# Three fp16 products of a value block: three matmuls of 128 columns into one PSUM region, in place of one of 256 and one of 128

## The chip, the cores and the metric

The kernel runs on one core of a Trainium2 chip. The metric is the device time of one execution in microseconds (us), from the first to the last instruction of that core and what the runtime puts around it; less is better. TensorE is PE in the profile (PEld is its weight loads), VectorE is DVE, ScalarE is ACT, GpSimd is POOL, and SP issues the transfers.

## The reference

Two layers of graph attention on 3125 nodes with 128 features, 103125 edges, then a residual and a layer norm. Of one layer (4 heads in the first, 2 in the second, 128 features per head):

```python
q = (x @ Wq + bq).reshape(n, H, C)
k = (x @ Wk + bk).reshape(n, H, C)
v = (x @ Wv + bv).reshape(n, H, C)
alpha = jnp.einsum('ehc,ehc->eh', q[dst], k[src]) / jnp.sqrt(jnp.float32(C))
amax = jax.ops.segment_max(alpha, dst, num_segments=n)
p = jnp.exp(alpha - amax[dst])
denom = jax.ops.segment_sum(p, dst, num_segments=n) + 1e-16
out = jax.ops.segment_sum(p[:, :, None] * v[src], dst, num_segments=n)
out = out / denom[:, :, None]
return out.reshape(n, H * C) + x @ Ws + bs      # second layer: the mean over heads
```

The last step is `_layernorm(x + layer2(relu(layer1(x))))`.

## The kernel before

**Stages.** The kernel turns the edge list into a dense additive mask of 3125 x 3125 (the logarithm of the edge count), stored in DRAM (`mask_and_projections`, to 612 us of the span). `attention` then runs for layer 1 (612 to 1800 us), `projections2` between (1800 to 1925), `attention` for layer 2 (1925 to 2558), and `layer_norm` last.

**Attention.** Nodes are cut into NT = 25 tiles of TP = 125. For a tile of targets t and a head h, called head step s = t * H + h (100 of them in layer 1, 50 in layer 2), the 3125 sources are cut into NP = 7 pieces: six of 500 (four tiles) and one of 125 (one tile). For each piece PE makes the scores (three fp16 products of high and low parts, L1239), DVE adds the mask and takes the maximum (L1133), ACT takes the exponential (L1077), PE transposes the probabilities tile by tile (L1264, fp32), ACT writes their high fp16 part (L1084), DVE their low part (L1145), and PE sums the values (`values`, L1268 to L1279). So there are 25 value tiles in a head step, 3750 in all, in 1050 blocks of four tiles or of one.

**Precision.** K, V, the queries and the probabilities are held as a high and a low fp16 part. Of a product of two such pairs three terms are kept: high x high, high x low, low x high. In `values` the first matmul has the high probabilities as its weights and the high and low V side by side as 256 moving columns (L1275), so that high x high goes to columns 0 to 127 of the PSUM bank `O` and high x low to columns 128 to 255. The second has the low probabilities as weights and the high V as 128 moving columns (L1277), into columns 0 to 127. Each `pe.matmul` is a weight load of 125 columns and a matmul. There is one bank `O`: the first value block of a head step waits for `s_sum` of the step before (L1271).

**After the seven pieces** DVE runs `value_sum` (L1166): it waits for the last value matmul, copies the low half of `O` to `summed` (L1170, semaphore `s_low`) and adds the high half (L1172, `s_sum`). POOL multiplies by `v_back`, the powers of two that undo the scaling of V (L1038, `s_back`), then by the softmax weight (L1041), and adds the skip rows (L1047, or L1050 and L1053 in layer 2).

**What sets the order.** Each engine's order is written out by hand in its `tile` function, one step k = 0..6 per piece. PE issues in a step: the scores of the piece k + 5, the transposes of the piece k + 2 (both ahead, into the next head steps), then the values of piece k. DVE issues: mask and maximum of the piece k + 5, at k = 6 `value_sum`, then the low part of the piece k + 2, then small softmax operations. `over_tiles` (L958) runs the first tile, then a hardware loop of 11 passes with two tiles in each (L961), then the last two tiles. The waits are semaphores; none of the other ones is touched.

Of the kernel before, what the change touches and what calls it, by code (L numbers as in the profile page):

```python
# [22 lines left out]
ALU = mybir.AluOpType  # L23
# [5 lines left out]
TP = 125  # L29
NT = N // TP  # L30
C = 128
# [50 lines left out]
def wait(eng, sem, value):  # L82

    if not (isinstance(value, int) and value <= 0):
        eng.wait_ge(sem, value)


def tiles_of(p):

    return range(PIECES[p][0] // TP, PIECES[p][1] // TP)  # L90


def build(nc, x, src, dst, Wq1, bq1, Wk1, bk1, Wv1, bv1, Ws1, bs1,
# [4 lines left out]
    with ExitStack() as ctx:  # L98
# [6 lines left out]
        with ExitStack() as lay:  # L105
            def sb1(name, shape, dt=F32):
                return lay.enter_context(nc.sbuf_tensor(name, shape, dt))

            layer1 = {
                "featT": sb1("xT", [C, NT, 1, TP]),  # L110
                "KT": sb1("KT1", [C, H1, 2, N], F16),
                "V": sb1("V1", [TP, NT, H1, 2, C], F16),
                "v_back": sb1("v_back1", [C, H1 * C]),
                "Wq": sb1("Wq1_sb", [C, 1, H1 * C]),
                "Ws": sb1("Ws1_sb", [C, 1, H1 * C]),
                "bq": sb1("bq1_sb", [C, H1]),
                "bs": sb1("bs1_sb", [TP, H1 * C]),
            }
            mask_and_projections(nc, x, src, dst, Wk1, bk1, Wv1, bv1, Wq1, bq1, Ws1, bs1, bs2,
                                 ident, xres, layer1, mask_dram)  # L120
            attention(nc, 1, H1, 1, layer1, mask_dram, ident, hT_dram=hT_dram, h_max=h_max)
# [783 lines left out]
def attention(nc, layer, H, KC, L, mask_dram, ident, hT_dram=None, h_max=None, xres=None, y=None, stats=None):  # L905
# [3 lines left out]
    featT, KT, V, v_back, Wq, Ws, bq = (L[n] for n in ("featT", "KT", "V", "v_back", "Wq", "Ws", "bq"))  # L909
    W = H * C if layer == 1 else C  # L910
    with ExitStack() as ctx:
        def sb(name, shape, dt=F32):
            return ctx.enter_context(nc.sbuf_tensor(f"{name}_l{layer}", shape, dt))

        def bank(name):
            return ctx.enter_context(nc.psum_tensor(f"{name}_l{layer}", [C, 512], F32))

        def sem(name):
            return ctx.enter_context(nc.semaphore(f"{name}_l{layer}"))
# [16 lines left out]
        summed = sb("summed", [TP, 2, C])  # L936
# [3 lines left out]
        O, B_q, B_skip = bank("output"), bank("query"), bank("skip_rows")  # L940
# [6 lines left out]
        s_max, s_exp = sem("max_ready"), sem("exp_ready")  # L947
        s_tp, s_hi, s_t = sem("transposed_in_psum"), sem("probT_hi_ready"), sem("probT_ready")
        s_pv = sem("values_summed")
        s_sum, s_back, s_wtd, s_out = (sem(n) for n in ("sum_ready", "sum_scaled_back", "sum_weighted", "rows_ready"))  # L950
        s_low, s_pool_seen, s_top = sem("sum_low_ready"), sem("pool_seen"), sem("largest_taken")
        s_sp, s_skip = sem("skip_in_psum"), sem("skip_ready")
        s_rp, s_r, s_stored = sem("rowsT_in_psum"), sem("rowsT_ready"), sem("rowsT_stored")
        s_tot, s_w0, s_w1, s_w2 = (sem(n) for n in ("total_ready", "denom_ready", "inverse_ready", "weight_ready"))
# [3 lines left out]
        def over_tiles(eng, body):  # L958

            body(0, 0, 0)  # L960
            with eng.Fori(0, (NT - 3) // 2) as i:  # L961
                body(2 * i + 1, i, 1)
                body(2 * i + 2, i + 1, 0)
            body(NT - 2, (NT - 2) // 2, 1)
            body(NT - 1, (NT - 1) // 2, 0)
# [4 lines left out]
        def exists(t):  # L970
            return not isinstance(t, int) or t < NT

        def ahead(t, h, n):

            return t + (h + n) // H, (h + n) % H
# [13 lines left out]
        with nc.Block() as block:  # L989
            @block.sync  # L990
            def _(sp):
                def load_mask(t, parity):
                    for r0, r1 in ROW_SPLIT:
                        sp.dma_start(mask[r0:r1, parity, :], mask_dram[bass.ds(t * TP + r0, r1 - r0), :]
                                     ).then_inc(s_mask[parity], 16)

                def store_rowsT(t):
                    sp.wait_ge(s_r, t + 1)
                    sp.dma_start(hT_dram[bass.ds(t, 1)].rearrange("a p n -> (a p) n"), rowsT[:, :]).then_inc(s_stored, 16)

                def tile(t, i, parity):
                    if exists(t + 2):
                        sp.wait_ge(s_masked, NP * H * (t + 1))
                        load_mask(t + 2, parity)
                    if layer == 1:
                        store_rowsT(t)

                for n, (a, b) in enumerate(FIRST):
                    for r0, r1 in ROW_SPLIT:
                        sp.dma_start(mask[r0:r1, 0, a:b], mask_dram[r0:r1, a:b]).then_inc(s_first[n], 16)  # L1010
                load_mask(1, 1)
                over_tiles(sp, tile)
                if layer == 1:
                    sp.wait_ge(s_stored, 16 * NT)

            @block.gpsimd
            def _(pool):
                def query_parts(n, u):

                    pool.wait_ge(s_qs, n + 1).then_inc(s_pool_seen, 1)
                    pool.tensor_copy(QT[:, u, 0, :], q_now[:, u, :]).then_inc(s_qh, 1)  # L1023
                    pool.wait_ge(s_qh, n + 1)
                    pool.tensor_tensor(QT[:, u, 1, :], q_now[:, u, :], QT[:, u, 0, :], ALU.subtract).then_inc(s_q, 1)

                def tile(t, i, parity):
                    wait(pool, s_sp, t)
                    pool.tensor_copy(feat_now[:, :, :].rearrange("c k n -> c (k n)"),
                                     featT[:, bass.ds(t, 1), :, :].rearrange("c a k n -> c (a k n)")).then_inc(s_feat, 1)  # L1030
                    for h in range(H):
                        s = t * H + h
                        if exists(ahead(t, h, 3)[0]):
                            query_parts(s + 3, (h + 3) % 2)

                        o = summed[:, h % 2, :]
                        pool.wait_ge(s_sum, s + 1)
                        pool.tensor_tensor(o, o, v_back[0:TP, h * C:(h + 1) * C], ALU.mult).then_inc(s_back, 1)  # L1038
                        pool.wait_ge(s_w2, s + 1)
                        pool.wait_ge(s_back, s + 1).then_inc(s_pool_seen, 1)  # L1040
                        pool.tensor_scalar(o, o, weight[:, h % 2:h % 2 + 1], None, ALU.mult).then_inc(s_wtd, 1)  # L1041
                        pool.wait_ge(s_skip, t + 1)
                        pool.wait_ge(s_wtd, s + 1)
                        if layer == 1:
                            if h == 0:
                                wait(pool, s_rp, t)
                            pool.tensor_tensor(rows[:, h * C:(h + 1) * C], o, skip[:, h * C:(h + 1) * C],  # L1047
                                               ALU.add).then_inc(s_out, 1)
                        elif h == 0:
                            pool.tensor_tensor(rows[:, :], o, skip[:, :], ALU.add).then_inc(s_out, 1)  # L1050
                        else:
                            pool.wait_ge(s_out, s)
                            pool.tensor_tensor(y[:, bass.ds(t, 1), :].rearrange("p a c -> p (a c)"), o, rows[:, :],  # L1053
                                               ALU.add).then_inc(s_out, 1)

                for n in range(3):
                    query_parts(n, n % 2)
                over_tiles(pool, tile)

            @block.scalar  # L1060
# [56 lines left out]
            def _(dve):  # L1117
# [48 lines left out]
                def value_sum(s, h):  # L1166

                    dve.wait_ge(s_pv, NP * (s + 1))
                    wait(dve, s_out, s - 1)
                    dve.tensor_copy(summed[:, h % 2, :], O[0:TP, C:2 * C]).then_inc(s_low, 1)  # L1170
                    dve.wait_ge(s_low, s + 1)
                    dve.tensor_tensor(summed[:, h % 2, :], O[0:TP, 0:C], summed[:, h % 2, :], ALU.add).then_inc(s_sum, 1)  # L1172

                def largest_features(t):
                    dve.wait_ge(s_r, t + 1)
# [45 lines left out]
            def _(pe):  # L1221
# [46 lines left out]
                def values(s, p, h):  # L1268
                    pe.wait_ge(s_t, NP * s + p + 1)
                    if p == 0:  # L1270
                        wait(pe, s_sum, s)  # L1271
                    for i, t in enumerate(tiles_of(p)):
                        hi, lo = (probT[:, p, n, i * TP:(i + 1) * TP] for n in range(2))

                        pe.matmul(O[0:TP, 0:2 * C], hi, V[:, t, h, :, :].rearrange("p a c -> p (a c)"),  # L1275
                                  start=t == 0, stop=False, skip_group_check=True)
                        last = pe.matmul(O[0:TP, 0:C], lo, V[:, t, h, 0, :], start=False, stop=t == NT - 1,  # L1277
                                         skip_group_check=True)
                    last.then_inc(s_pv, 1)  # L1279
# [93 lines left out]
```

## Time and profile before

| | |
|---|---|
| time, median of 3 runs | 2584.7 us (2581.99 to 2587.41) |
| span of the profiled execution | 2580.9 us |
| mean granted PE clock | 0.978 |
| PE, PEld busy | 2360.8, 2004.2 us |
| DVE, ACT, POOL busy | 2026.2, 1651.1, 433.0 us |
| attention, layer 1 and layer 2 | 612 to 1800 us and 1925 to 2558 us |
| `values`: matmuls of 256 and of 128 columns | 3750 and 3750 |
| value matmuls' busy time | 739.8 and 680.9 us |

The page gives no time of its own for the profiled execution beside the span; the median of the runs is 3.8 us above the span. PE's busy time counts pipelined matmuls that overlap, so the cost of a matmul is read from the distance between two starts, not from its duration.

### The profile page before, as it was taken

Reading aid. Unit: us, or ns where it says so; the run is one execution under the profiler, and the core shown is the slowest. Engines: PE = TensorE matmul, PEld = TensorE weight load, DVE = VectorE, ACT = ScalarE, POOL = GpSimd, SP = SyncE. Lnnn points to the kernel's source line nnn. Section 1 sums busy time; section 2 is a strip of 40 time slices with the busy share of each in tenths; the row PEclk is TensorE's granted clock in tenths of the full one; section 3 lists DMA queues with packets and bytes.
Section 4 is the critical chain, followed back from the end, with each engine's and each line's share of the span. In section 5 each row is a group of like instructions: output and inputs, shape, how many; then the busy total and the mean of one; then the engine's idle time right before and its main releaser. Section 6 shows DMA issues by size and latency. Waiting matters only on the chain. (4 is left out here: it accounts for less than half of the span.)

```text
span 2580.9 us, 64168 instructions
## 1 busy us (share of the span) xinstructions
PE 2360.8 (91%) x18557; PEld 2004.2 (78%) x18558; DVE 2026.2 (79%) x6021; ACT 1651.1 (64%) x3383; POOL 433.0 (17%) x876
## 2 busy tenths in 40 slices
PE   2778888887999999999999999998789999999995
PEld 1356666666888888888888888888468999999995
DVE  5699999997888878888878878887237777777775
ACT  1689999995666666666666666665116665566653
POOL 4410000000211111121212111121011121211211
PEclk8889999999999999999999999999899999999998
DMA  2012222223211211112112112110312221222210
GB/s 71 1 59 87 87 86 86 86 86 93 54 31 33 55 34 36 48 34 54 30 34 54 30 34 54 33 31 9 134 42 68 63 73 48 73 60 61 73 48 26
DMA packets 46697, 141.98 MB, mean 55 GB/s; under 512 B 7621, under 2 KB 22828, under 8 KB 40249
## 3 DMA queue, kind: packets, MB, share of 16 engines
q1 hardware_dynamic: 43103, 136.94, 19.1%
q10 hardware_dynamic: 3396, 2.42, 0.4%
q8 instruction: 121, 1.98, 0.3%
q14 instruction: 77, 0.63, 0.1%
HBM read 91.34 MB, written 48.00 MB: 54 GB/s over the span
## 5 line engine op out<-in xcount | busy, mean ns | idle before, releaser
L1084 ACT ACTIVATE probT_l<-transposed_l 125x500 f16<-125x500 f32 (+1 forms) x1050 | 569.7, 543 | 669.5 <-PE transposed_l L1264 655.2
L1133 DVE CUSTOM_DVE_ANT_0 prob_l<-score_l,mask_l 125x500 f32<-125x500 f32 (+1 forms) x1050 | 649.8, 620 | 256.1 <-PE score_l L1239 210.6
L1239 PE MATMUL score_l<-KT,QT_l 128*125 128x500 f16 (+1 forms) x3150 | 771.1, 354 | 24.1 <-issue 17.6
L1145 DVE SCALAR_TENSOR_TENSOR probT_l<-transposed_l,probT_l 125x500 f16<-125x500 f32 (+1 forms) x1050 | 651.0, 620 | 125.4 <-ACT probT_l L1084 119.3
L1275 PE MATMUL output_l<-V,probT_l 125*125 125x256 f16 x3750 | 739.8, 275 | 0.0
L1277 PE MATMUL output_l<-V,probT_l 125*125 125x128 f16 x3750 | 680.9, 219 | 0.0
L1264 PEld LDWEIGHTS transposed_l<-ident,prob_l 125*125 125x125 f32 x3750 | 549.5, 188 | 91.8 <-DVE probT_l L1145 6.7
L1264 PE MATMUL transposed_l<-ident,prob_l 125*125 125x125 f32 x3750 | 589.5, 275 | 5.0 <-DVE probT_l L1145 5.0
L1077 ACT ACTIVATE prob_l<-prob_l,neg_max_l 125x1000 f32<-125x1000 f32 (+1 forms) x450 | 521.5, 1159 | 0.0
L1275 PEld LDWEIGHTS output_l<-V,probT_l 125*125 125x125 f16 x3750 | 512.3, 137 | 9.7 <-issue 0.2
L1277 PEld LDWEIGHTS output_l<-V,probT_l 125*125 125x125 f16 x3750 | 516.9, 138 | 0.0
L739 PE MATMUL mask_banks<-hot,work 125*125 125x313 bf16 x2432 | 388.4, 307 | 66.6 <-DVE hot L646 66.2
L1239 PEld LDWEIGHTS score_l<-KT,QT_l 128*125 128x125 f16 x3150 | 347.9, 138 | 113.6 <-issue 36.0
L739 PEld LDWEIGHTS mask_banks<-hot,work 125*125 125x125 bf16 x2432 | 278.8, 136 | 158.7 <-DVE hot L646 67.1
L646 DVE TENSOR_SCALAR hot<-cols,col_of 125x626 bf16<-125x626 f16 x960 | 316.3, 371 | 1.4 <-PE mask_banks L739 1.4
L1023 POOL CAST QT_l<-q_now_l 128x125 f16<-128x125 f32 x150 | 43.8, 292 | 1276.0 <-ACT q_now_l L1064 1276.0
L416 ACT ACTIVATE row_diff<-rows,minus_rel 125x125 bf16<-125x125 f16 x640 | 211.0, 389 | 8.9 <-DVE minus_rel L633 6.8
L1038 POOL TENSOR_TENSOR summed_l<-summed_l,v_back 125x128 f32<-125x128 f32 x150 | 68.2, 455 | 595.6 <-DVE summed_l L1172 595.6
L426 ACT ACTIVATE work<-row_diff,one 125x250 bf16<-125x250 bf16 x320 | 151.5, 494 | 0.0
L644 DVE TENSOR_SCALAR work<-rows,row_of,base 125x250 bf16<-125x250 f16 (+1 forms) x320 | 105.2, 329 | 0.9 <-PE mask_banks L739 0.9
L624 DVE SCALAR_TENSOR_TENSOR work<-mask_banks,work 125x626 f32<-125x626 f32 x128 | 101.6, 794 | 1.8 <-ACT work L400 1.8
L400 ACT ACTIVATE work<-mask_banks,tiny 125x626 f32<-125x626 f32 x128 | 98.6, 770 | 4.0 <-PE mask_banks L748 3.5
(176 smaller groups left out, 1723.2 us busy)
## 6 DMA issues: line engine op xcount, KB each, us to landing
mask_l<-mask_scratch SPq DMA_DIRECT2D x48, 1367.2 KB
mask_scratch<-work SPq DMA_DIRECT2D x128, 273.4 KB
mask_l<-mask_scratch SPq DMA_DIRECT2D x48, 158.7 KB
hT_scratch<-rowsT_l SPq DMA_DIRECT2D x25, 250.0 KB, 2.2
hT<-hT_scratch SPq DMA_DIRECT2D x6, 1000.0 KB, 13.5
mask_scratch<-work SPq DMA_DIRECT2D x128, 31.7 KB
mask_l<-mask_scratch SPq DMA_DIRECT2D x2, 929.7 KB
xres<-in_x SPq DMA_DIRECT2D x1, 1562.5 KB
```

The costliest lines, as they stand in the source:

```text
L416: last = act.activation(row_diff[:, n % 3, start:end], rows[:, cut], ACT.Square, bias=minus_rel[:, u, k:k + 1])
L426: act.activation(row_buffer[:, start:start + width(n)], row_diff[:, n % 3, 0:width(n)], ACT.Relu, bias=one[:, 0:1], scale=-1.0).then_inc(s ...
L646: dve.tensor_scalar(col_hot[:, k % RING, :], cols[:, :], col_w[:, k:k + 1], BIG, ALU.is_equal, ALU.mult).then_inc(s_hot, 1)
L739: ins = pe.matmul(counts(u, v)[:, a, :], one_hot, col_hot[:, hot, a * HB:(a + 1) * HB], start=k == (0, KF1)[v], stop=False, skip_group_che ...
L1077: act.activation(e, e, ACT.Exp, bias=neg_max[:, h % 2:h % 2 + 1], accum_out=total[:, h % 2, c:c + 1]).then_inc(s_exp, 1)
L1084: act.activation(probT[:, p, 0, 0:b - a], flip_bank(h, p)[0:TP, 0:b - a], ACT.Copy, scale=P_UP).then_inc(s_hi, 1)
L1133: dve.tensor_tensor_reduce(out=prob[:, h % 2, a:b], in0=score_bank(h, p)[0:TP, 0:b - a], in1=mask[:, parity, a:b], scale=1.0, scalar=-3.0e ...
L1145: dve.scalar_tensor_tensor(probT[:, p, 1, 0:b - a], flip_bank(h, p)[0:TP, 0:b - a], P_UP, probT[:, p, 0, 0:b - a], ALU.mult, ALU.subtract) ...
L1239: last = pe.matmul(score_bank(h, p)[0:TP, 0:b - a], QT[:, h % 2, i, :], KT[:, h, j, a:b], start=n == 0, stop=n == len(parts) - 1)
L1264: last = pe.transpose(flip_bank(h, p)[0:TP, i * TP:(i + 1) * TP], prob[:, h % 2, t * TP:(t + 1) * TP], ident[0:TP, 0:TP])
L1275: pe.matmul(O[0:TP, 0:2 * C], hi, V[:, t, h, :, :].rearrange("p a c -> p (a c)"), start=t == 0, stop=False, skip_group_check=True)
L1277: last = pe.matmul(O[0:TP, 0:C], lo, V[:, t, h, 0, :], start=False, stop=t == NT - 1, skip_group_check=True)
```

## The change

The two matmuls of a value tile become three of 128 columns, all into columns 0 to 127 of `O`: high x high, high x low (with the high probabilities loaded as weights a second time), low x high. With all three terms in one place, DVE's copy of the low half, its semaphore and the addition go: DVE now multiplies `O` by `v_back` in one instruction, and POOL's multiplication by `v_back` goes. POOL's next instruction waits for `s_sum` directly.

```diff
-        s_sum, s_back, s_wtd, s_out = (sem(n) for n in ("sum_ready", "sum_scaled_back", "sum_weighted", "rows_ready"))
-        s_low, s_pool_seen, s_top = sem("sum_low_ready"), sem("pool_seen"), sem("largest_taken")
+        s_sum, s_wtd, s_out = (sem(n) for n in ("sum_ready", "sum_weighted", "rows_ready"))
+        s_pool_seen, s_top = sem("pool_seen"), sem("largest_taken")
@@ attention, gpsimd, tile @@
                         o = summed[:, h % 2, :]
-                        pool.wait_ge(s_sum, s + 1)
-                        pool.tensor_tensor(o, o, v_back[0:TP, h * C:(h + 1) * C], ALU.mult).then_inc(s_back, 1)
                         pool.wait_ge(s_w2, s + 1)
-                        pool.wait_ge(s_back, s + 1).then_inc(s_pool_seen, 1)
+                        pool.wait_ge(s_sum, s + 1).then_inc(s_pool_seen, 1)
                         pool.tensor_scalar(o, o, weight[:, h % 2:h % 2 + 1], None, ALU.mult).then_inc(s_wtd, 1)
@@ attention, vector, value_sum @@
                     dve.wait_ge(s_pv, NP * (s + 1))
                     wait(dve, s_out, s - 1)
-                    dve.tensor_copy(summed[:, h % 2, :], O[0:TP, C:2 * C]).then_inc(s_low, 1)
-                    dve.wait_ge(s_low, s + 1)
-                    dve.tensor_tensor(summed[:, h % 2, :], O[0:TP, 0:C], summed[:, h % 2, :], ALU.add).then_inc(s_sum, 1)
+                    dve.tensor_tensor(summed[:, h % 2, :], O[0:TP, 0:C], v_back[0:TP, h * C:(h + 1) * C], ALU.mult).then_inc(s_sum, 1)
@@ attention, tensor, values @@
                         hi, lo = (probT[:, p, n, i * TP:(i + 1) * TP] for n in range(2))
 
-                        pe.matmul(O[0:TP, 0:2 * C], hi, V[:, t, h, :, :].rearrange("p a c -> p (a c)"),
-                                  start=t == 0, stop=False, skip_group_check=True)
+                        pe.matmul(O[0:TP, 0:C], hi, V[:, t, h, 0, :], start=t == 0, stop=False, skip_group_check=True)
+                        pe.matmul(O[0:TP, 0:C], hi, V[:, t, h, 1, :], start=False, stop=False, skip_group_check=True)
                         last = pe.matmul(O[0:TP, 0:C], lo, V[:, t, h, 0, :], start=False, stop=t == NT - 1,
                                          skip_group_check=True)
```

## Rows read from the trace of the kernel before

**Rows 1.** The page: busy time by engine, and slices of the span.

```profile
PE 2360.8 (91%) x18557; PEld 2004.2 (78%) x18558; DVE 2026.2 (79%) x6021; ACT 1651.1 (64%) x3383; POOL 433.0 (17%) x876
...
PE   2778888887999999999999999998789999999995
```

**Rows 2.** Stretches: window, its length, busy us (instructions) by engine, PE clock, DMA share, GB/s.

```profile
612.00:1800.00 1188.00, 1166.15 (x9941) 1037.93 (x9942) 962.45 (x2847) 749.26 (x1424) 225.86 (x520) 1.00 0.15 40
...
1925.00:2558.00 633.00, 622.38 (x5393) 564.74 (x5392) 470.91 (x1450) 375.81 (x701) 125.32 (x275) 1.00 0.24 62
954.20:1049.20 95.00, 92.94 (x798) 82.95 (x797) 77.12 (x229) 59.92 (x114) 18.24 (x42) 1.00 0.15 40
2116.00:2165.60 49.60, 49.60 (x435) 45.22 (x434) 37.68 (x117) 29.98 (x56) 10.04 (x22) 1.00 0.25 63
```

**Rows 3.** Waits: engine and line, for whom; us in total, times, longest us.

```profile
POOL summed_l L1038 <- DVE summed_l L1172: 595.6, 150, 9.1
DVE prob_l L1133 <- PE score_l L1239: 210.6, 424, 2.7
...
PE score_l L1239 <- issue: 17.6, 10, 2.1
```

**Rows 4.** Timeline of PE, layer 1: start us, length us, engine, line, what.

```profile
1015.48 0.80 PE L1239 MATMUL score_l<-KT,QT_l 128*125 128x500 f16 x3
1016.11 0.60 PE L1264 MATMUL transposed_l<-ident,prob_l 125*125 125x125 f32 x4
1016.59 0.29 PE L1275 MATMUL output_l<-V,probT_l 125*125 125x256 f16 x1
1016.72 0.22 PE L1277 MATMUL output_l<-V,probT_l 125*125 125x128 f16 x1
1016.77 0.27 PE L1275 MATMUL output_l<-V,probT_l 125*125 125x256 f16 x1
1016.88 0.22 PE L1277 MATMUL output_l<-V,probT_l 125*125 125x128 f16 x1
...
1017.22 0.22 PE L1277 MATMUL output_l<-V,probT_l 125*125 125x128 f16 x1
1017.27 0.34 PE L1239 MATMUL score_l<-KT,QT_l 128*125 128x125 f16 x3
1017.45 0.65 PE L1264 MATMUL transposed_l<-ident,prob_l 125*125 125x125 f32 x4
```

**Rows 5.** Timeline of PE, two other head steps, the 125-column scores and what follows.

```profile
1028.55 0.34 PE L1239 MATMUL score_l<-KT,QT_l 128*125 128x125 f16 x3
1028.72 0.54 PE L1264 MATMUL transposed_l<-ident,prob_l 125*125 125x125 f32 x3
...
1099.14 0.34 PE L1239 MATMUL score_l<-KT,QT_l 128*125 128x125 f16 x3
1099.31 0.43 PE L1264 MATMUL transposed_l<-ident,prob_l 125*125 125x125 f32 x2
```

**Rows 6.** The page, costliest groups: two weight loads of PE, and POOL's multiplication.

```profile
L1275 PEld LDWEIGHTS output_l<-V,probT_l 125*125 125x125 f16 x3750 | 512.3, 137 | 9.7 <-issue 0.2
...
L1239 PEld LDWEIGHTS score_l<-KT,QT_l 128*125 128x125 f16 x3150 | 347.9, 138 | 113.6 <-issue 36.0
...
L1038 POOL TENSOR_TENSOR summed_l<-summed_l,v_back 125x128 f32<-125x128 f32 x150 | 68.2, 455 | 595.6 <-DVE summed_l L1172 595.6
```

**Rows 7.** Timeline of DVE around one value sum.

```profile
1015.83 0.28 DVE L1170 COPY summed_l<-output_l 125x128 f32<-125x128 f32 x1
1016.15 0.29 DVE L1172 TENSOR_TENSOR summed_l<-output_l,summed_l 125x128 f32<-125x128 f32 x1
```

**Rows 8.** Timeline of PE where layer 1's loop starts a new pass.

```profile
1049.22 0.22 PE L1277 MATMUL output_l<-V,probT_l 125*125 125x128 f16 x1
1050.94 0.84 PE L1239 MATMUL score_l<-KT,QT_l 128*125 128x500 f16 x3 [1.50 <-issue]
```

**Rows 9.** DMA queues, one pass of layer 1's loop: kind, packets, MB, share.

```profile
q8 instruction: 9, 0.15, 0.7%
```

**Rows 10.** DMA queues, 2020 to 2520 us (layer 2's loop): all that moved.

```profile
DMA packets 3080, 31.25 MB, mean 63 GB/s; under 512 B 580, under 2 KB 580, under 8 KB 580
## 3 DMA queue, kind: packets, MB, share of 16 engines
q1 hardware_dynamic: 3080, 31.25, 24.5%
```

## The prediction

> **What bounds the kernel.** I first read the page's busy shares and slices [rows 1]: PE is in tenths 9 nearly throughout the two attention stages, DVE, ACT and POOL are not. The stretches [rows 2] say how long these stages are: 1188 us and 633 us, together 1821 of the span of 2580.9 us, at a granted clock of 1.00 (the 2.4 GHz level), with DVE busy for 81% and 74%. The waits [rows 3] say who is late: DVE waited 210.6 us for PE's scores and POOL 595.6 us for DVE's sums, while the one large wait of PE in these stages, 17.6 us in 10 places, is at the turns of layer 1's loop. So in attention every nanosecond by which PE's stream of matmuls grows or shrinks is a nanosecond of the kernel, and DVE or POOL time that is saved is worth nothing by itself; it counts only where PE waits for it. The change touches nothing outside attention.
>
> A matmul's price is the distance between starts in the timeline of PE [rows 4]. Value tiles go at 1016.77 to 1017.27, three tiles in 0.50 us: **167 ns a tile**, of which the 256 columns take 0.11 and the 128 columns 0.055 us. At 2.4 GHz, 384 columns are 160 ns, so PE now pays almost nothing but columns: each weight load is hidden behind the matmul ahead of it.
>
> **Part 1, three matmuls a tile.** The columns stay 384. What is added is a matmul and a weight load per tile, 3750 of each. The second load of the same weights is not skipped: the scores too use the same query part twice in a row, and show 3150 loads [rows 6], three a piece in 1050 pieces. The question is what a load and a matmul of 128 columns cost in a row, with no 256-column matmul to hide a load.
>
> The nearest rows are the scores of the last piece: three loads of 125 fp16 columns with matmuls of 125. From their first start to the first transpose behind them is 0.18 us in [rows 4] and 0.17 us in each of the two places of [rows 5], so 174 ns for three: **58 ns a pair**, though 125 columns alone are 52 ns. Why it is the load that costs: behind these short matmuls the four fp32 transposes take 0.65 us, against 0.60 us behind the 500-column scores [rows 4]. The first fp32 load was not covered by a matmul of 125 fp16 columns; so loads have a pace of their own. An fp32 pair costs (0.60 - 0.27) / 3 = 110 ns, and half of that is 55 ns for fp16. The lower bound is then the 55 to 56 ns between a 128-column value matmul and its successor (1017.22 to 1017.27), when a load has had slack before; the upper one is 59 ns, the reading 0.18 us / 3 and rounding. The far end is one weight load per pair without overlap, 137 ns [rows 6]; I exclude it, since the 58 ns rows already have one in each pair. A gain in this part is excluded by the columns, which are as many.
>
> I take 58, as these rows are the same instruction forms but for 3 columns: 3 x 58 = 174 ns a tile, 7 more than 167, times 3750 = +26 us. The first pair of each of the 1050 blocks has slack from the transposes, some 2 ns: -2 us. **Part 1: +24 us**, with ends of +4 us (56 ns) and +37 us (59 ns).
>
> In the Trainium skill, "TensorE: Matmul & The Clock Gate", section "Back-to-back issue gap", a stream of load and matmul pairs is said to sustain about 81 ns each at 128 columns. By that rule a tile would be 243 ns and part 1 +285 us; the 58 ns of the rows disagree with it, over three pairs in a row.
>
> That three matmuls in a row add into the same 128 columns costs nothing new: the low matmul and the next high one already meet there 55 ns apart [rows 4], and so do the three scores.
>
> **Part 2, DVE's copy.** 150 copies of 0.28 us with the hand-over behind them go; from the copy's start to the addition's is 0.32 us [rows 7], so 48 us leave DVE. The new multiplication reads PSUM and SBUF as the addition did, 0.29 us, and I leave it at that (bounds: the copy's 0.28, and this). DVE waits for PE anyway, so 48 us are worth nothing there. But PE waits for `s_sum` at the first value block of a head step. The addition ends at 1016.44 [rows 7], and the first value matmul starts at 1016.59 [rows 4]: the last transpose started at 1016.11 + 0.60 - 0.27 = 1016.44, and its successor without a wait comes 0.11 later, so 0.04 us are lost. The next distance is 0.13 and not 0.11 us, so another 0.02: PE's sequencer stood at the wait and had no instructions queued ahead. That is 0.06 us in 150 head steps, 9 to 10 us. With the sum 0.32 us earlier the wait is gone five times over. What is late next is the stream of PE itself. **Part 2: -9 us**, bounds 0 (if the hand-over has some other releaser) and -15 us (0.10 us a step).
>
> **Part 3, POOL.** 150 multiplications of 455 ns go; POOL's wait moves from the first to the second instruction. Nothing is queued behind it that was not queued behind the old wait, and POOL stood idle for 595.6 us before L1038 [rows 6], in wait of that sum. Rows come 0.32 + 0.46 us earlier, and the skip sums and row transposes that need them were not late in [rows 3]. Nothing. If the cover went, it would be a gain.
>
> **Part 4, longer code.** Each turn of layer 1's loop shows a hole of 1.72 us from start to start, 1.50 us idle, ended by "issue" [rows 8], with 9 fetches of instructions in a pass [rows 9]: PE runs its queued work out while the code of the loop's head is fetched. The queue then holds a fixed number of instructions, and they will on average be shorter in time: a pass of 95 us has 798 matmuls, and will have 998 [rows 2], so what covers the hole shrinks by a fifth. I take the cover at about 1 us, an estimate from the 1.1 us that lie between 1015.48 and 1016.59 [rows 4], the scores and transposes that ran on while PE's sequencer stood at a wait: +0.2 us a turn, 10 turns, **+2 us** (0 to +5).
>
> **Sum:** +24 - 9 + 2 = +17 us on the span of 2580.9, so 2598. The median of the runs is 3.8 us over the span, 2584.7 us; with the same around it the forecast is **2601 us**.
>
> **Rivals.** *(B) Faster or level: the pair is as cheap as its columns.* If the 58 ns come from the odd width of 125 and not from the load, or if the second load of the same weights costs nothing, a tile is 3 x 56 = 168 ns and part 1 is +4 us. Then the wait removed in part 2 decides: +4 - 9 + 2 = -3, 2582 us; with part 2 at its end of -15 it is 2576. The turning point of the whole change is a pair of (167 + 7 / 3.75) / 3 = 56.3 ns. For it: 56 ns behind a 128-column matmul is in the rows. Against it: that load had slack, and the transposes of [rows 4] show loads with a pace of their own.
>
> *(C) Layer 2's loop outgrows the instruction store.* It fetches no instructions at all from 2020 to 2520 us [rows 10], and its passes of 435 matmuls have no hole, while layer 1's with 798 have [rows 2, 8]. A pass will have 535. The limit lies between 435 and 798; if below 535, ten turns get a hole of 1.7 us each: +17 us more, 2618 us. Against it: 535 is at 28% of that way.
>
> In the Trainium skill, "Runtime: NRT & Kernel Launch", section "Instruction fetch mechanics", PE's store holds 2048 instructions, refilled in blocks of 256. By it a pass of 535 loads, 535 matmuls and their waits, some 1150 instructions by my estimate, would still fit, and case C would add 0 us; that 1600 and more already miss agrees only if blocks fetched ahead push out the loop's head.
>
> *(D) The pairs cannot be fed.* If the present mean of 167 / 2 = 83.5 ns a pair is what PE's instruction supply sustains, and the 58 ns only a burst out of its queue, a tile is 250 ns: +83 x 3750 = +313 us, 2891 us. This is the skill's 81 ns as a mechanism of this kernel. Against it: PE's queue visibly ran ahead where nothing blocked it, and in a step of 19 pairs only 12 are short.
>
> **How the numbers follow.** My forecast (A), pairs at 57 to 59 ns, gets 0.68 with its own range of 2590 to 2612 us; B 0.19, C 0.08, D 0.05. D, with a few hundredths of A's and C's edges, is left out: the range is 2577 to 2620 us. A measurement of this kernel can tell a change from none at about 0.2%, 5.2 us. Faster by more is the better half of B, 0.10; within it are the rest of B and the edge of A with a pair near 57 and a larger gain in part 2, 0.18; slower is the rest, 0.72.
>
> **What would show it.** In the profile of the changed kernel: four tiles of values in about 0.70 us where now 0.67 (B: 0.67, D: 1.0); value matmuls 11250, all of 128 columns, and as many loads; 0.11 us from the last transpose to the first value matmul of a head step, next distance 0.06; DVE without L1170 and 48 us less busy; ten holes of 1.7 to 2 us in layer 1 and none in layer 2, with no instruction fetches between 2020 and 2520 us. Wrong would be a tile under 169 ns, fetches in layer 2's loop, or a wait of PE for DVE in the place of that for `s_sum`.

## The result and the profile after

| | before | after |
|---|---|---|
| median | 2585.5 us (2581.99 to 2587.41) | 2605.6 us (2604.35 to 2607.55) |
| ratio | | 1.008, 95% interval 1.0066 to 1.0095 |
| span of the profiled execution | 2580.9 us | 2603.4 us |

The changed kernel is slower by 0.8%, 20.1 us by the medians; the two profiled executions lie 22.5 us apart. 2601 with a range of 2577 to 2620 was forecast. The page of the changed kernel, busy time by engine and four of its costliest groups:

```profile
PE 2381.7 (91%) x22307; PEld 2029.5 (78%) x22308; DVE 2000.4 (77%) x5871; ACT 1655.5 (64%) x3383; POOL 364.6 (14%) x726
...
L1272 PE MATMUL output_l<-V,probT_l 125*125 125x128 f16 x3750 | 702.9, 222 | 0.0
L1273 PE MATMUL output_l<-V,probT_l 125*125 125x128 f16 x3750 | 702.4, 222 | 0.0
L1271 PE MATMUL output_l<-V,probT_l 125*125 125x128 f16 x3750 | 701.1, 221 | 0.0
...
L1271 PEld LDWEIGHTS output_l<-V,probT_l 125*125 125x125 f16 x3750 | 518.3, 138 | 4.3
```

All that was meant to go is gone: DVE has 150 instructions less than in [rows 1], POOL 150 instructions and 68 us less, and the time rose. DVE's busy time fell by 26 us only, where the prediction had 48: the copies that went took 43 us by their durations and the hand-over behind them the rest of the 48, but the instructions left overlap less with their neighbours than before. 3750 matmuls and 3750 loads came in their place; the second load of the same weights is a full one. Busy shares say little here: PE's busy time rose by 21 us only, since overlapped durations are counted once.

The timeline of PE after the change, a value block of four tiles (one tile is L1271, L1272 and L1273):

```profile
1201.67 0.60 PE L1260 MATMUL transposed_l<-ident,prob_l 125*125 125x125 f32 x4
1202.10 0.22 PE L1271 MATMUL output_l<-V,probT_l 125*125 125x128 f16 x1
1202.16 0.22 PE L1272 MATMUL output_l<-V,probT_l 125*125 125x128 f16 x1
1202.22 0.22 PE L1273 MATMUL output_l<-V,probT_l 125*125 125x128 f16 x1
1202.28 0.22 PE L1271 MATMUL output_l<-V,probT_l 125*125 125x128 f16 x1
...
1202.45 0.22 PE L1271 MATMUL output_l<-V,probT_l 125*125 125x128 f16 x1
...
1202.62 0.22 PE L1271 MATMUL output_l<-V,probT_l 125*125 125x128 f16 x1
...
1202.80 0.80 PE L1235 MATMUL score_l<-KT,QT_l 128*125 128x500 f16 x3
```

Four tiles take 1202.10 to 1202.80, 0.70 us, 175 ns each by these rounded starts. From all starts inside blocks a tile takes 173.3 ns on average, against 167.5 ns before; the three distances in it are 57.5, 58.0 and 58.2 ns where they were 111.4 and 55.9.

Now the first value block of a head step, with DVE's sum ahead of it (to be held against [rows 4, 7]). First DVE, then PE:

```profile
1193.03 0.29 DVE L1168 TENSOR_TENSOR summed_l<-output_l,v_back 125x128 f32<-125x128 f32 x1
```

```profile
1193.31 0.60 PE L1260 MATMUL transposed_l<-ident,prob_l 125*125 125x125 f32 x4
1193.75 0.22 PE L1271 MATMUL output_l<-V,probT_l 125*125 125x128 f16 x1
1193.80 0.22 PE L1272 MATMUL output_l<-V,probT_l 125*125 125x128 f16 x1
```

The sum is ready at 1193.03 + 0.29 = 1193.32, as the transposes begin. The first value matmul follows the last transpose (1193.31 + 0.60 - 0.27 = 1193.64) by 0.11 us, and the next comes 0.055 later: no wait. It is gone in nine of ten head steps; in each of the 11 passes of layer 1's loop one step still has a late sum, which costs some 0.07 us.

The waits of PE in the attention stages, and the place behind one turn of layer 1's loop:

```profile
PE score_l L1235 <- issue: 20.8, 10, 2.5
```

```profile
1154.99 0.22 PE L1273 MATMUL output_l<-V,probT_l 125*125 125x128 f16 x1
1157.20 0.84 PE L1235 MATMUL score_l<-KT,QT_l 128*125 128x500 f16 x3 [1.99 <-issue]
```

The ten holes of [rows 3, 8], the stretches in which PE starts nothing, are longer: from start to start 2.31 us on average where it was 1.98. Behind the longest, of 2.68 us, the granted clock falls, from 1350.3 to 1353.7 us:

```profile
1350.30:1353.70 3.40, 3.40 (x28) 3.40 (x28) 1.82 (x6) 0.85 (x2) 0.00 (x0) 0.50 0.01 2
```

PE's granted clock (the third number from the end) is 0.50 there, the 1.2 GHz level. Layer 1's loop has two such stretches after the change, behind holes of 2.68 and of 2.09 us, and had one before, behind one of 2.20.

**Where the 22.5 us between the two spans lie.** Layer 1's attention starts 2.3 us later, in a part that the change does not touch. From there to the first projection of layer 2 it is 16.4 us more, from there to the last value matmul 4.7 us more, and 0.9 us less in the rest.

### The profile page after: what moved, and what is told of

The parts are those of the page before. It is cut to its first block and busy times, and to the rows that moved or that the text cites. A ratio compares the mean times of both kernels' runs of the same rounds, so it can differ in the third digit from the quotient of the medians.

```text
span 2603.4 us, 71368 instructions
## 1 busy us (share of the span) xinstructions
PE 2381.7 (91%) x22307; PEld 2029.5 (78%) x22308; DVE 2000.4 (77%) x5871; ACT 1655.5 (64%) x3383; POOL 364.6 (14%) x726
## 5 line engine op out<-in xcount | busy, mean ns | idle before, releaser
L1272 PE MATMUL output_l<-V,probT_l 125*125 125x128 f16 x3750 | 702.9, 222 | 0.0
L1273 PE MATMUL output_l<-V,probT_l 125*125 125x128 f16 x3750 | 702.4, 222 | 0.0
L1271 PE MATMUL output_l<-V,probT_l 125*125 125x128 f16 x3750 | 701.1, 221 | 0.0
L1271 PEld LDWEIGHTS output_l<-V,probT_l 125*125 125x125 f16 x3750 | 518.3, 138 | 4.3
L1273 PEld LDWEIGHTS output_l<-V,probT_l 125*125 125x125 f16 x3750 | 519.3, 138 | 0.0
L1272 PEld LDWEIGHTS output_l<-V,probT_l 125*125 125x125 f16 x3750 | 517.6, 138 | 0.0
L1039 POOL TENSOR_SCALAR summed_l<-summed_l,weight_l 125x128 f32<-125x128 f32 x150 | 90.9, 606 | 589.3 <-DVE summed_l L1168 589.3
```

What stands on the lines that cost most here:

```text
L1271: pe.matmul(O[0:TP, 0:C], hi, V[:, t, h, 0, :], start=t == 0, stop=False, skip_group_check=True)
L1272: pe.matmul(O[0:TP, 0:C], hi, V[:, t, h, 1, :], start=False, stop=False, skip_group_check=True)
```

## The experiments

**One part at a time.** First the matmuls alone, with DVE and POOL as before:

```diff
-                        pe.matmul(O[0:TP, 0:2 * C], hi, V[:, t, h, :, :].rearrange("p a c -> p (a c)"),
-                                  start=t == 0, stop=False, skip_group_check=True)
+                        pe.matmul(O[0:TP, 0:C], hi, V[:, t, h, 0, :], start=t == 0, stop=False, skip_group_check=True)
+                        pe.matmul(O[0:TP, C:2 * C], hi, V[:, t, h, 1, :], start=False, stop=False, skip_group_check=True)
```

> The first part of the change alone: three matmuls of 128 columns a tile, but high x low still goes to columns 128 to 255, and the copy, the addition and POOL's multiplication stay. Theory (loads set the pace of short pairs): a tile takes 173 ns, where before it took 167, so +22 to +24 us for the 3750 tiles, +2 to +4 us at the turns of layer 1's loop, and the wait for s_sum stays at 0.06 us a head step: 2608 to 2613 us, 5 to 10 us slower than the changed kernel. Rival 1 (three sums into the same 128 columns in a row cost something): a tile falls back to 167 or 168 ns and the time to about 2590 us. Rival 2 (the chain on DVE and POOL gave nothing): 2605 us, as the changed kernel.

Measured: 2615.2 us against 2583.2, ratio 1.012 (1.0104 to 1.0135), +32 us and 9.7 us over the changed kernel. (The changed kernel was timed in another round than these trials; the kernel before has medians of 2585.5 and 2583.2 us in the two, so distances to the changed kernel are good to some 2 us.) The median tile is 173 ns, so rival 1 falls: where the sums go plays no part. Against rival 2 stand the 10 us, but not all of them are the chain on DVE and POOL. The time is 2 us above my upper end. The holes are 2.27 us, and in layer 1's loop five of them are followed by the 1.2 GHz level, where the changed kernel has two and the kernel before one. In layer 2, where the clock is 1.00 throughout, this trial is 3.2 us over the changed kernel (rows further down), so rival 2 does fall.

Then DVE and POOL alone, on the two matmuls of before:

```diff
-                    dve.tensor_copy(summed[:, h % 2, :], O[0:TP, C:2 * C]).then_inc(s_low, 1)
-                    dve.wait_ge(s_low, s + 1)
-                    dve.tensor_tensor(summed[:, h % 2, :], O[0:TP, 0:C], summed[:, h % 2, :], ALU.add).then_inc(s_sum, 1)
+                    dve.tensor_tensor(summed[:, h % 2, :], O[0:TP, 0:C], v_back[0:TP, h * C:(h + 1) * C], ALU.mult).then_inc(s_sum, 1)
...
-                        pool.wait_ge(s_sum, s + 1)
-                        pool.tensor_tensor(o, o, v_back[0:TP, h * C:(h + 1) * C], ALU.mult).then_inc(s_back, 1)
                         pool.wait_ge(s_w2, s + 1)
-                        pool.wait_ge(s_back, s + 1).then_inc(s_pool_seen, 1)
+                        pool.wait_ge(s_sum, s + 1).then_inc(s_pool_seen, 1)
```

> The second part alone: two matmuls of 256 and 128 columns as before, and DVE and POOL as in the changed kernel. The product of the high probabilities and the low V is computed and left out of the result. Theory: the wait of PE for s_sum goes, 0.06 us in 150 head steps, and nothing else moves: 9 to 10 us faster than before, about 2576 us, a ratio of 0.996. Rival 1 (the wait had another releaser): no change. Rival 2 (the load taken off DVE and POOL counts too): 15 us or more faster.

Measured: 2574.1 us, ratio 0.9961 (0.9948 to 0.9975), -9.2 us, with the product high x low left out of the result. So 48 us of DVE and 68 us of POOL are worth about the 9 us that PE waited for the sum.

**What makes a pair 58 ns.** Fewer weight columns, as many moving ones (the last 29 rows of a tile lack two of the three products):

```diff
-                        pe.matmul(O[0:TP, 0:C], hi, V[:, t, h, 1, :], start=False, stop=False, skip_group_check=True)
-                        last = pe.matmul(O[0:TP, 0:C], lo, V[:, t, h, 0, :], start=False, stop=t == NT - 1,
+                        pe.matmul(O[0:96, 0:C], hi[:, 0:96], V[:, t, h, 1, :], start=False, stop=False, skip_group_check=True)
+                        last = pe.matmul(O[0:96, 0:C], lo[:, 0:96], V[:, t, h, 0, :], start=False, stop=t == NT - 1,
                                          skip_group_check=True)
```

> The changed kernel with 96 in place of 125 weight columns in the second and third matmul of a tile; moving columns stay 128. The last 29 rows of each tile lack high x low and low x high. Theory (a load's time goes with its columns, and sets the pace): these pairs cost their 128 columns again, 56 ns, a tile 167 to 169 ns, and the time is 15 to 20 us under the changed kernel's, 2586 to 2590 us. Rival (a pair costs 58 ns whatever it loads, a price of the instruction or of the matmul): the tile stays at 173 ns, the time at 2605 us.

Measured: 2588.1 us, ratio to before 1.002 (1.0011 to 1.0029), 17.5 us under the changed kernel. Its timeline of PE:

```profile
1201.51 0.22 PE L1271 MATMUL output_l<-V,probT_l 125*125 125x128 f16 x1
1201.57 0.22 PE L1272 MATMUL output_l<-V,probT_l 125*96 125x128 f16 x1
1201.62 0.22 PE L1273 MATMUL output_l<-V,probT_l 125*96 125x128 f16 x1
1201.68 0.22 PE L1271 MATMUL output_l<-V,probT_l 125*125 125x128 f16 x1
...
1202.18 0.38 PE L1235 MATMUL score_l<-KT,QT_l 128*125 128x500 f16 x1
```

0.67 us for four tiles as before the change; the mean tile is 168.9 ns. Each matmul still streams 128 columns; only two of three loads are shorter. The matmuls behind them also write 96 rows in place of 125, but that is not the price: in the kernel before, matmuls with 125 rows and 128 columns are followed after 55.9 ns. So the price follows the load.

Then the reverse, fewer moving columns and full loads (the last 16 features lack two of the three products):

```diff
-                        pe.matmul(O[0:TP, 0:C], hi, V[:, t, h, 1, :], start=False, stop=False, skip_group_check=True)
-                        last = pe.matmul(O[0:TP, 0:C], lo, V[:, t, h, 0, :], start=False, stop=t == NT - 1,
+                        pe.matmul(O[0:TP, 0:112], hi, V[:, t, h, 1, 0:112], start=False, stop=False, skip_group_check=True)
+                        last = pe.matmul(O[0:TP, 0:112], lo, V[:, t, h, 0, 0:112], start=False, stop=t == NT - 1,
                                          skip_group_check=True)
```

> The changed kernel with 112 in place of 128 moving columns in the second and third matmul of a tile; weight columns stay 125. The last 16 features lack high x low and low x high. Theory (the loads set the pace): these pairs cost no less than 57 ns, a tile 171 to 173 ns, the time 0 to 8 us under the changed kernel's, 2597 to 2605 us. Rival (a pair costs its columns and some 4 ns): 16 columns less are 6.7 ns less in two of three pairs, a tile 160 ns, and the time 50 us under the changed kernel's, 2555 us.

Measured: 2601.0 us, ratio to before 1.0072 (1.0056 to 1.0087), 4.6 us under the changed kernel. Its timeline of PE:

```profile
1201.54 0.23 PE L1271 MATMUL output_l<-V,probT_l 125*125 125x128 f16 x1
1201.61 0.21 PE L1272 MATMUL output_l<-V,probT_l 125*125 125x112 f16 x1
1201.66 0.22 PE L1273 MATMUL output_l<-V,probT_l 125*125 125x112 f16 x1
1201.72 0.23 PE L1271 MATMUL output_l<-V,probT_l 125*125 125x128 f16 x1
...
1201.89 0.23 PE L1271 MATMUL output_l<-V,probT_l 125*125 125x128 f16 x1
```

0.35 us for two tiles. The distances inside a tile move to 62, 51 and 58 ns, their sum is 172 ns: 32 columns less, 13 ns of stream at 2.4 GHz, take 2 ns off. Even these are lost again, as the scores behind a block come 194 ns apart on average, where it was 190: layer 2's attention takes as long as in the changed kernel (next rows). With loads of 125 fp16 columns in a row a pair costs 57 to 58 ns, with 112 moving columns as with 128. The rival is out.

**One stretch without holes.** Layer 2's attention has no hole and no fall of the clock in the kernel before, in the changed one and in the four trials above, so its length shows PE's stream alone. These rows give, for the last matmul of a tile in layer 2, count, duration in ns and first and last start; kernel before, changed kernel, then the trials in their order:

```profile
L1277 PE MATMUL output_l<-V,probT_l x1250: 217/219/219, 1945.6 to 2554.8; 125*125 125x128 f16 x179
L1273 PE MATMUL output_l<-V,probT_l x1250: 221/222/222, 1964.2 to 2578.1; 125*125 125x128 f16 x179
L1277 PE MATMUL output_l<-V,probT_l x1250: 220/222/223, 1971.8 to 2588.9; 125*125 125x128 f16 x179
L1273 PE MATMUL output_l<-V,probT_l x1250: 217/219/220, 1941.8 to 2547.6; 125*125 125x128 f16 x179
L1273 PE MATMUL output_l<-V,probT_l x1250: 218/219/220, 1954.7 to 2563.5; 125*96 125x128 f16 x179
L1273 PE MATMUL output_l<-V,probT_l x1250: 220/222/223, 1957.0 to 2571.0; 125*125 125x112 f16 x179
```

That is 609.2, 613.9, 617.1, 605.8, 608.8 and 614.0 us. Three matmuls a tile cost 617.1 - 609.2 = 7.9 us on the old chain and 613.9 - 605.8 = 8.1 us on the short one, or 6.4 ns a tile; the short chain gives back 3.2 to 3.4 us in 50 head steps, some 66 ns a step. Shorter loads take 5.1 of the 8.1 us off again, fewer moving columns nothing. What the other 3.0 us are, the one load of 125 columns that stayed or the added matmul itself, is not taken apart. The stretch repeats to 0.1 us: with layer 1 in straight code, further down, it is 609.2 and 613.9 us again.

**A value sum that keeps the cheap stream.** On the kernel before:

```diff
-                    dve.tensor_copy(summed[:, h % 2, :], O[0:TP, C:2 * C]).then_inc(s_low, 1)
-                    dve.wait_ge(s_low, s + 1)
-                    dve.tensor_tensor(summed[:, h % 2, :], O[0:TP, 0:C], summed[:, h % 2, :], ALU.add).then_inc(s_sum, 1)
+                    dve.tensor_reduce(summed[:, h % 2, :], O[0:TP, 0:2 * C].rearrange("p (a c) -> p c a", a=2),
+                                      AX.X, ALU.add).then_inc(s_sum, 1)
```

> The kernel before, two matmuls a tile, with DVE's copy and addition in one reduction over the two halves of the bank: 256 elements read in pairs 128 apart. The result is complete. Theory: the reduction takes 0.40 to 0.45 us (0.285 for 128 elements and 128 more at about 1 ns), 0.15 to 0.2 us less than copy and addition, which is more than the 0.06 us that PE waits; so this keeps the cheap stream and loses the wait: 9 to 10 us faster than before, about 2576 us, and as fast as the part that touches DVE and POOL alone. Rival (reading PSUM in steps is slow, 0.6 us or more): no change.

Measured: 2580.1 us against 2586.6, ratio 0.9973 (0.9963 to 0.9983), -6.5 us. Its group of DVE:

```profile
L1170 DVE TENSOR_REDUCE summed_l<-output_l 125x128 f32<-125x256 f32 x150 | 63.0, 420 | 1.7 <-PE output_l L1276 1.6
```

420 ns as expected. The distance from the last transpose to the first value matmul is 109 ns in the median, no wait, but 126 ns on average: in 11 steps, one in each pass of layer 1's loop, the sum is late for another reason, and there the shorter head start is missed, by some 0.2 us each. These 2.4 us are as much as is missing of the 9. The nine executions fall into 2576 to 2577 and 2580 to 2582 us, though, and the traced one is of the lower group, so the agreement is not proof.

**The loop's turns.** Layer 1 in straight code, on the kernel before and on the changed one:

```diff
         def over_tiles(eng, body):
 
+            if layer == 1:
+                for t in range(NT):
+                    body(t, t // 2, t % 2)
+                return
             body(0, 0, 0)
```

> The kernel before, with layer 1's 25 tiles written out and no hardware loop there; layer 2 keeps its loop. Theory (the holes come from the jump back, behind which code must be fetched; straight code is fetched ahead): the ten holes of 1.7 to 2.3 us go, 19 us, and the one short fall of the clock with them: 17 to 22 us faster than before, 2563 to 2568 us. Rival (code is fetched too slowly in any case, or a tile's turn itself makes the hole): no change, or slower.

Measured: 2564.1 us against 2586.6, ratio 0.992 (0.9905 to 0.9935), -22.5 us. PE has no wait for "issue" in attention any more, and the stretch 612 to 1780 us reads:

```profile
612.00:1780.00 1168.00, 1163.64 (x9941) 1037.92 (x9939) 961.99 (x2847) 748.63 (x1423) 224.98 (x519) 1.00 0.15 40
```

The same 9941 matmuls as in the first of [rows 2] fit into 1168 us instead of 1188.

> The changed kernel with layer 1's tiles written out. Theory: its ten holes are 0.3 us longer than before and now two falls of the clock hang on them; without all that the changed kernel is 15 to 17 us slower than the kernel before treated in the same way, 2580 to 2584 us, where with the loops it is 20 us slower. Rival (the larger part of the 20 us has nothing to do with the loop): the difference of the two written-out kernels is 20 us or more.

Measured: 2575.0 us, ratio to before 0.996 (0.9945 to 0.9975). It is 10.9 us over the other written-out kernel by the medians, 12.8 us by the spans. The expectation of 15 to 17 was too high: 20.1 - 10.9 = 9 us hang on the loop by the medians. Layer 1's attention alone, from its first to its last value matmul, says less: the change makes it 16.2 us longer with the loop (1172.6 to 1188.8) and 9.9 us longer in straight code (1151.8 to 1161.7), so 6.4 us are the loop's. Without it no sum is late either: 109 ns from the last transpose to the first value matmul in every step.

> Both finds together on the kernel before: one reduction for the value sum, and layer 1's tiles written out. The result is complete. Theory: the gains add, 9 to 10 and 17 to 22 us: 2553 to 2559 us. Rival: with the holes gone DVE is later and they add to less, 2563 us or more.

Measured: 2553.7 us against 2586.6, ratio 0.9881 (0.9866 to 0.9896), -33 us, with the full result. It is 10.4 us under the kernel that is only written out, so in straight code the reduction brings the whole of PE's wait. This version beats both kernels.

**Is it the length of the code?** The kernel before, with layer 2's loop made longer:

```diff
-            with eng.Fori(0, (NT - 3) // 2) as i:
-                body(2 * i + 1, i, 1)
-                body(2 * i + 2, i + 1, 0)
+            if layer == 2:
+                with eng.Fori(0, 5) as j:
+                    for m in range(4):
+                        body(4 * j + m + 1, 2 * j + (m + 1) // 2, (m + 1) % 2)
+                body(21, 10, 1)
+                body(22, 11, 0)
+            else:
+                with eng.Fori(0, (NT - 3) // 2) as i:
+                    body(2 * i + 1, i, 1)
+                    body(2 * i + 2, i + 1, 0)
```

> The kernel before, with four tiles in place of two in a pass of layer 2's loop: 5 passes of some 870 matmuls instead of 11 of 435, then four tiles in straight code. Layer 1 is untouched. Theory (the holes come from the length of the loop's code, which must be fetched anew at each jump back when it is long): layer 2 gets 4 holes of 1.7 to 2.3 us and fetches instructions throughout, where before it had no hole and no fetch: 7 to 10 us slower than before. Rival (the holes belong to layer 1's work, four heads and its row transposes, and not to the length): no hole, no change.

Measured: 2595.2 us against 2581.6, ratio 1.0052 (1.0035 to 1.0069), +13.6 us. Layer 2 has four holes, one of them here, and fetches instructions:

```profile
2168.75 0.22 PE L1284 MATMUL output_l<-V,probT_l 125*125 125x128 f16 x1
2171.04 0.84 PE L1246 MATMUL score_l<-KT,QT_l 128*125 128x500 f16 x3 [2.07 <-issue]
```

```profile
q8 instruction: 50, 0.82, 0.7%
```

That is for 2000 to 2540 us, where [rows 10] show no fetch at all from 2020 to 2520; 35 of the 50 fall within the loop, from 2020 to 2375. The holes are 2.2 to 2.5 us from start to start, and behind two of them the clock is at the 1.2 GHz level for 3.4 us: more than the 7 to 10 us that I expected, as the clock was not in my count.

## Why the prediction was right

**Direction and size.** The main forecast (A) came in: 20 us more by the medians, where 16 were forecast; 22.5 us by the spans, where the sum had 17.

**Part 1, +24 us.** The step "a pair of load and matmul costs 58 ns" was right, at the mean 57.8. The two means of a tile, 173.3 and 167.5 ns, give 5.8 ns, but the 167.5 hold a part of the wait of part 2 (with the short chain alone a tile is 166.4). The stretch of layer 2, where the chain is the same on both sides, gives 6.4 ns, times 3750 **+24 us**. The reading of the 125-column scores and of the transposes behind them [rows 4, 5] carried it, and two experiments that change one side of the pair each show that the load is the cause of most of it.

**Part 2, -9 us.** The part alone gave -9.2 us, and layer 2's 66 ns a head step are 10 us in 150. PE's distances across the wait went from 154 and 130 ns to 115 and 58 ns. That the saved DVE and POOL time by itself is worth next to nothing was right too.

**Part 3, nothing.** It was never apart from part 2 in a run, and it was not quite nothing: from the start of the last value matmul to the end of the span it is 26.1 us before, 25.3 us after the change and 25.9 us in the run with one reduction, which keeps POOL's multiplication. Behind the last tile no matmul covers POOL, and some 0.6 us of its time count.

**Part 4, +2 us (0 to +5).** This is the term that was mis-sized: layer 1's attention puts it at 6.4 us. The holes grew by 0.32 us each, where "+0.2 us a turn, 10 turns" stood, which is 3.2 us. Two items were not in the term at all: one more fall of the clock, which costs at most half of 3.4 us, 1.7, and 11 late sums of 0.07 us, 0.8. Together these are 5.7 of the 6.4 us. That the holes grow because PE's queue covers less time agrees with the runs, but was not shown: a pass also has more code to fetch, and no run has one without the other. They are 1.91 to 2.00 us in the traces with two matmuls a tile and 2.22 to 2.31 us in the four with three.

**What the sum hid.** The forecast was +24 - 9 + 2; measured are about +24 - 10 + 6. Add 2.3 us that came before the attention, in a part that the change does not touch, and most of the span's 22.5 us is accounted for. So the first two terms did not need luck, and nearly the whole miss is part 4.

**Rivals.** B asked for a pair under 56.3 ns; it was 57.8, and the trial with loads of 96 columns shows what B would have been: 168.9 ns a tile. C did not come: in the changed kernel, layer 2's loop from 2040 to 2536 us fetches nothing, and its passes go from 49.59 to 49.99 us without a hole. The run with four tiles a pass shows that the mechanism is real, between 535 matmuls a pass (none) and some 870 (holes). In the Trainium skill, "Runtime: NRT & Kernel Launch", section "Instruction fetch mechanics", a store of 2048 instructions and refills of 256 ahead of use are stated for PE; that 535 matmuls with as many loads fit agrees with it. That 798 and 870 matmuls a pass, with their loads still under 2048, do miss agrees only if blocks fetched ahead push out the loop's head, which no run shows. D did not come: twelve pairs in a row ran at 58 ns. The 81 ns that the Trainium skill, "TensorE: Matmul & The Clock Gate", section "Back-to-back issue gap", gives for such a stream are contradicted here.

## What to carry to other kernels

Where one engine's stream is the bound, price an edit by that stream first: here 116 us taken off DVE and POOL were worth 9 us, and one more weight load and matmul per tile, for the same columns, cost 24. Here matmuls of 128 moving columns did not quite hide loads of 125 fp16 columns in a row, and one of 256 did. So put the terms that share weights side by side in one wide matmul, and join them on the other engine in one instruction. To price such a change, take a stretch of the trace that has no hole and no fall of the clock, and compare its length in both kernels. And look at the turns of a hardware loop: where a pass fetched instructions here, each turn cost 2 us and sometimes a fall of the clock, and straight code was 22 us faster.

## What was not expected

- The long load shows in the distance behind its own matmul, not in the one ahead of it: in the kernel with loads of 125, 96 and 96 columns, the distance behind the matmul with the long load is 57.4 ns, the other two 55.9. Why is not shown.
- With 112 moving columns the three distances are 62, 51 and 58 ns: single distances shift, and their sum of 172, 2 ns under the full columns' 174, is made up for at the scores.
- A hole of 2.1 to 2.7 us in PE's stream is sometimes followed by 3.4 us at a granted clock of 0.50 (2 of 10 in the changed kernel, 5 of 10 in the one with split matmuls, 1 of 10 before). These are single executions, and the number varies between executions of the same code: with four tiles a pass in layer 2, layer 1 is as before, and none of its ten holes is followed by a fall. The spread of a kernel's times goes with it: of the kernel before, timed beside the trials, executions at a mean granted clock of 0.978 took 2579.3 to 2582.2 us, those at 0.975 or less 2586.5 to 2590.8. I cannot tell from these runs which holes are hit.
- Once in a pass of layer 1's loop DVE starts a masked maximum half a microsecond late (at 1204.15 us, with its semaphore seen at 1203.64 and nothing shown that it waits for), and with it the next value sum is late. In straight code no sum is late. Whether it is DVE's own fetch of instructions was not tried.
